# A transformer layer stack with an expert attention branch: a new order of each engine's work in an expert unit, and another opening

## What is computed

```python
xn = _layernorm(x, axis=-1)
x = x + encoder(xn, ...) + expert_attention(xn, ...)
```

```python
qs.append(jnp.einsum('bnm,dm->bnd', xm, q_w[:, :m]) + q_b)     # xm = xn[..., :m], m = d // 2 ** e
...
attn = softmax(einsum('bhqd,bhkd->bhqk', q, k) * scale);  out = einsum(attn, v) -> projection + x
```

## Time and profile before

| what | us |
|---|---|
| runs | 1592.49, 1591.91, 1586.09 (median 1591.91) |
| the profiled execution | 1587.46 |
| its span (first to last instruction) | 1585.5 |
| PE busy in the span | 1413.4 |
| ACT busy | 1219.2 |
| DVE busy | 1089.7 |
| POOL busy | 606.5 |

### The profile page before, as it was taken

The page is one execution under the profiler, slowest core; times in us unless marked ns, Lnnn a source line. Parts: engine busy times, 40 slices in busy tenths (PEclk is TensorE's granted clock), DMA queues, the critical chain, the costliest instruction groups (busy, mean ns, idle before and its releaser), DMA issues.

```text
span 1585.5 us, 39460 instructions
## 1 busy us (share of the span) xinstructions
PE 1413.4 (89%) x10594; PEld 941.7 (59%) x10720; DVE 1089.7 (69%) x2850; ACT 1219.2 (77%) x2165; POOL 606.5 (38%) x1052
## 2 busy tenths in 40 slices
PE   0677778669999999999999999999999999999995
PEld 0445555435666666666666666666666666666653
DVE  6576667456676777777777767767777777777762
ACT  3233333237899999999999989999999999999883
POOL 5232322223334333433333333334333345555433
PEclk9899988779999999999999999999999999999997
DMA  4333332144444444544444445444444554444430
GB/s 127 110 101 100 100 100 89 51 122 121 122 121 125 130 125 128 150 126 120 123 130 127 121 128 152 126 122 131 127 120 131 134 140 129 138 136 127 130 86 11
DMA packets 106534, 187.78 MB, mean 118 GB/s; under 512 B 20104, under 2 KB 72456, under 8 KB 106448
## 3 DMA queue, kind: packets, MB, share of 16 engines
q1 hardware_dynamic: 91632, 150.45, 34.4%
q0 software_dynamic: 14848, 36.72, 8.4%
HBM read 120.87 MB, written 65.01 MB: 117 GB/s over the span
## 4 chain that ended last, share of the span: by engine, by line
PE 69%; DVE 11%; issue 8%; DMA 5%; ACT 3%; POOL 1%; SPq 0%; DVEq 0%; POOLq 0%; ACTq 0%
PE pvp L1079 14%; PE exp_ps L1056 11%; DVE negm L772 10%; PE mxp L1022 10%; PE dense L1120 7%; PE mxp L968 5%; PE dense L997 5%; PE mxp L1026 4%; PE dense L1108 3%; PE dense L968 3%; PE mxp L1007 2%; PE mxp L1097 2%; DMA blocks<-negt 2%; PE mxp L1030 1%; DMA blocks<-split_L 1%
## 5 line engine op out<-in xcount | busy, mean ns | idle before, releaser
L922 ACT ACTIVATE probs<-exp_ps 128x512 f32<-128x512 f32 x896 | 512.1, 592 | 226.2 <-PE exp_ps L1056 221.7
L772 DVE TENSOR_REDUCE negm<-mxp 128x2 f32<-128x512 f32 x896 | 572.4, 686 | 77.3 <-PE mxp L1026 56.6
L1056 PE MATMUL exp_ps<-qbd_l,kst_l 128*128 128x512 f32 x768 | 346.8, 479 | 13.7 <-ACT exp_ps L947 9.7
L1022 PE MATMUL mxp<-blocks,qst 104*128 104x512 f32 x768 | 334.1, 468 | 4.9 <-DMA blocks<-split_L 4.2
L947 ACT ACTIVATE exp_ps<-masktf 128x512 f32<-128x512 f32 x513 | 308.7, 602 | 22.8 <-DVE rest L844 6.5
L596 POOL TENSOR_TENSOR lo<-y,hi 128x512 fp32r<-128x512 f32 x80 | 102.7, 1284 | 344.8 <-DVE hi L747 344.8
L1079 PE MATMUL pvp<-probs,vst_l 128*32 128x256 f32 (+1 forms) x4096 | 208.2, 333 | 10.6 <-issue 10.6
L1026 PE MATMUL mxp<-maskb,identb 128*128 128x256 bf16 (+1 forms) x642 | 197.8, 308 | 0.0
L1022 PEld LDWEIGHTS mxp<-blocks,qst 104*128 104x128 f32 x768 | 148.7, 194 | 46.3 <-issue 29.0
L1079 PEld LDWEIGHTS pvp<-probs,vst_l 128*32 128x32 f32 x4096 | 111.2, 110 | 95.8 <-issue 38.0
L1026 PEld LDWEIGHTS mxp<-maskb,identb 128*128 128x128 bf16 x768 | 75.2, 98 | 150.9 <-issue 137.7
(11 more groups left out here) (99 smaller groups left out, 1927.2 us busy)
## 6 DMA issues: line engine op xcount, KB each, us to landing
split_L<-hi SPq DMA_DIRECT2D x256, 128.0 KB, 2.1
qst<-split_L SPq DMA_DIRECT2D x64, 384.0 KB
kst_l<-split_L SPq DMA_DIRECT2D x64, 384.0 KB
qbd_l<-split_L SPq DMA_DIRECT2D x256, 96.0 KB
split_L<-lo POOLq DMA_DIRECT2D x128, 128.0 KB, 2.3
blocks<-split_L POOLq DMA_DIRECT2D x128, 96.0 KB, 4.3
blocks<-split_L SPq DMA_DIRECT2D x128, 96.0 KB
split_F<-hi SPq DMA_DIRECT2D x64, 128.0 KB, 2.1
```

Source lines behind the costliest of these rows:

```text
L772: dve.tensor_reduce(heads[:, g, first:first + count], bank[MAX_BANK + k % 3].rearrange("p (h t) -> p h t", h=count), AX.X, ALU.max, negate ...
L922: act.activation(probs[:, g, ch, :], exp_ps[:, k % 2, :], ACT.Exp, scale=plan.scale).then_inc(q.b_exp, 1)
L1022: pe.matmul(o, qst[0:BIAS_END, g, qt * P:(qt + 1) * P], kbd[0:BIAS_END, first:first + count, g, 0:keys], start=True, stop=True, skip_group ...
L1056: last = pe.matmul(o, kst[plan.name][:, s, g, kt * P:(kt + 1) * P], rhs, start=seeder not in ("ACT", "DVE"), stop=True, skip_group_check=True)
```

## The change

It has two parts. First, the expert slot is written anew: since each engine picks only its own steps out of the list, the new list gives each engine another order. Second, the opening loads the first quarter and the weights of the projections first, runs the statistics of two quarters and the norm of one, and starts the first unit; the rest is put between the first slots by a list of functions (`between`).

```diff
@@ Plan.slot_steps (two of its new rows)
-            + at("negt negt+ row>", s + 1) + part("pv", s, 2)
-            + part("pv", s, 3) + at("pv+", s) + at("stack> stackp", s + 2))
+                at("rstd ln", s + 2) + at("v+", s + 1) + at("op", s - 2) + at("stack>", s + 1) + at("hi>", s + 2)
+                + at("pv+", s - 1) + at("row> v", s + 1) + at("xn", s + 2) + at("ot+", s - 1) + at("xt+", s + 2)
@@ EXPERT
-    "xt": 1, "qk": 1, "v": 0, "at": 1, "op": 0, "negt": 1, "ot": 4})
+    "xt": 2, "qk": 2, "v": 1, "at": 0, "op": 4, "negt": 3, "ot": 0})
@@ expert_rounds
-    experts(-1)
-    experts(0)
-    experts(1)
+    for k, (n, slots) in enumerate(((-1, (0,)), (-1, (1,)), (0, (0, 1)), (1, (0, 1)))):
+        experts(n, slots=slots)
+        if between[k] is not None:
+            between[k]()
@@ SP
+            load_quarter(0)
+            for dst, src in ((wa["F"], wa_f), (seg_rows, seg_in)):
+                sp.dma_start(dst[:], src).then_inc(s_w_first, 16)
+            sp.dma_start(constant[0], rows_kf).then_inc(s_rows_first, 16)
+            load_quarter(1)
...
+            load_quarter(2)
+            load_quarter(3)
@@ POOL
-            pool.memset(blocks[:].bitcast(F32), 0.0).then_inc(s_zero, 1)
...
-            for k in range(4):
+            for k in range(2):
                 inverse_deviation_of_quarter(k, k + 1)
...
+            def clear_queries(k):
+                pool.memset(qbd["L"][0:ALIBI_ROW, k // 2, 8 * (k % 2):8 * (k % 2) + 8, :].bitcast(F32), 0.0).then_inc(s_initv, 1)
...
+            def second_half_of_deviations():
+                for k in range(2, 4):
+                    inverse_deviation_of_quarter(k, k + 1)
+                clear_queries(0)
...
+            expert_rounds(pool, experts, encoder, join,
+                          (None, second_half_of_deviations, lambda: clear_queries(1), lambda: clear_queries(2)))
@@ DVE
-            dve.memset(qbd["L"][0:ALIBI_ROW, :, :, :].bitcast(F32), 0.0).then_inc(s_initv, 1)
+            dve.memset(blocks[:].bitcast(F32), 0.0).then_inc(s_zero, 1)
...
+            expert_rounds(dve, experts, encoder, join,
+                          (lambda: first_norm(1), second_half_of_statistics, second_half_of_norms, None))
@@ ACT
+            act.wait_ge(s_rows_first, 16)
+            round_rows(0)
+            act.wait_ge(s_w_first, 16 * 2)
...
+            expert_rounds(act, experts, encoder, lambda: wait_for_projections(act, S["F"]),
+                          (round_other_rows, None, None, None))
```

More of the change, by code:

```diff
@@ L108, in slot_steps @@
         return (
[L109 to L115, removed]
-            + at("negt negt+ row>", s + 1) + part("pv", s, 2)
-            + part("pv", s, 3) + at("pv+", s) + at("stack> stackp", s + 2))
+                at("rstd ln", s + 2) + at("v+", s + 1) + at("op", s - 2) + at("stack>", s + 1) + at("hi>", s + 2)
+                + at("pv+", s - 1) + at("row> v", s + 1) + at("xn", s + 2) + at("ot+", s - 1) + at("xt+", s + 2)
+                + at("at+ ot", s - 1) + at("xt", s + 2)
+                + part("exp", s, 0, 1) + at("at", s - 1) + at("qk", s + 2) + part("pv", s, 0) + at("y", s + 2)
+                + at("xb", s - 2)
+                + part("exp", s, 2, 3) + at("op+", s - 2) + at("lo hi", s + 2) + part("max", s + 1, 0)
+                + at("stackp", s + 2) + part("max", s + 1, 1)
+                + part("exp", s, 4) + part("max", s + 1, 2, 3)
+                + part("exp", s, 5, 6) + part("max", s + 1, 4, 5) + part("pv", s, 1) + part("max", s + 1, 6)
+                + part("exp", s, 7) + part("max", s + 1, 7) + part("pv", s, 2, 3) + at("negt+ negt", s + 1))
     def steps(self, n, last_layer=False, slots=(0, 1), early=None):
@@ L224, in wait_for_projections, with expert_rounds @@
         eng.wait_ge(q.lo_parts[s], 16 * 2 * EXPERT.rounds)
-def expert_rounds(eng, experts, encoder, join):
-    experts(-1)
-    experts(0)
-    experts(1)
+def expert_rounds(eng, experts, encoder, join, between=(None, None, None, None)):
+    for k, (n, slots) in enumerate(((-1, (0,)), (-1, (1,)), (0, (0, 1)), (1, (0, 1)))):
+        experts(n, slots=slots)
+        if between[k] is not None:
+            between[k]()
     with eng.Fori(2, EXPERT.rounds - 1) as n:
@@ L673, in encoder, with join @@
                 steps(ENCODER, n, **part_of_round)
-            expert_rounds(pool, experts, encoder, lambda: wait_for_projections(pool, S["F"]))
+            def clear_queries(k):
[4 more added lines that the diff above has]
+                clear_queries(0)
+            def join():
+                clear_queries(3)
+                pool.wait_ge(s_w, 16 * 3)
+                wait_for_projections(pool, S["F"])
+            expert_rounds(pool, experts, encoder, join,
+                          (None, second_half_of_deviations, lambda: clear_queries(1), lambda: clear_queries(2)))
             pool.wait_ge(S["F"].b_s, EXPERT.exp_chunks * GROUPS * EXPERT.units)
@@ L709, in first_norm, with quarter_statistics @@
                     last.then_inc(s_norm, 1)
-            for k in range(4):
+            def quarter_statistics(k):
                 dve.wait_ge(s_x[k], 16)
@@ L714, in _ @@
                 statistics_of_quarter(rest, k, k + 1)
[L715 to L718, removed]
+            quarter_statistics(0)
+            quarter_statistics(1)
+            first_norm(0)
+            dve.wait_ge(s_w_first, 16 * 2)
             def statistics(q, stage, u, s, source):
@@ L882, in join, with second_half_of_statistics, second_half_of_norms @@
                 dve.sem_inc(S["L"].c_done, BATCH)
-            expert_rounds(dve, experts, encoder, join)
+            def second_half_of_statistics():
+                quarter_statistics(2)
+                quarter_statistics(3)
+                dve.wait_ge(s_w, 16 * 3)
+            def second_half_of_norms():
+                first_norm(2)
+                first_norm(3)
+            expert_rounds(dve, experts, encoder, join,
+                          (lambda: first_norm(1), second_half_of_statistics, second_half_of_norms, None))
             dve.wait_ge(S["F"].c_done, BATCH)
@@ L889, in _, with round_rows @@
         def _(act):
[L891 to L895, removed]
+            def round_rows(k):
+                for s in range(2):
+                    stack = (kst["F"], kst["L"], qbd["L"])[k]
+                    act.activation(stack[ALIBI_ROW:P, s, :, :].rearrange("p h t -> p (h t)"), constant[k], ACT.Copy)\
+                        .then_inc(s_rounded, 1)
+            act.wait_ge(s_rows_first, 16)
+            round_rows(0)
+            act.wait_ge(s_w_first, 16 * 2)
             def steps(plan, n, last_layer=False, **part_of_round):
@@ L954, in encoder, with round_other_rows @@
                 steps(ENCODER, n, **part_of_round)
-            expert_rounds(act, experts, encoder, lambda: wait_for_projections(act, S["F"]))
+            def round_other_rows():
+                act.wait_ge(s_rows, 16 * 2)
+                round_rows(1)
+                round_rows(2)
+            expert_rounds(act, experts, encoder, lambda: wait_for_projections(act, S["F"]),
+                          (round_other_rows, None, None, None))
             act.wait_ge(S["F"].c_done, BATCH)
@@ L1143, in _, with others_loaded @@
             pe.wait_ge(s_init, 12)
[L1144 to L1147, removed]
+            pe.wait_ge(s_zero, 3)
+            pe.wait_ge(s_rounded, 2)
+            pe.wait_ge(s_w_first, 16 * 2)
+            def others_loaded():
+                pe.wait_ge(s_rounded, 6)
+                pe.wait_ge(s_w, 16 * 3)
+            expert_rounds(pe, experts, encoder, lambda: wait_for_projections(pe, S["F"]),
+                          (None, others_loaded, None, None))
             pe.wait_ge(s_ones, 1)
```

13 lines of the change are left out of this document (8 added, 5 removed).

## The result

| | median us | range | ratio to before (95%) |
|---|---|---|---|
| before | 1591.91 | 1586.09 to 1592.49 | |
| after | 1578.90 | 1577.21 to 1580.70 | 0.9931 [0.9909, 0.9953] |

What follows compares the result with a forecast made beforehand. No engine was full; a chain of waits and the low clock set the slot. Slots minus 16.1, opening minus 0.9, end plus 1.0 made minus 16.0 us: 1571.5 for the profiled execution, 1575 by the median, range 1560 to 1589.

Steps and rivals of the forecast that it cites:

- The slot at full clock: Expert slot in the new order: 14.7 us against 15.7 at full clock, 1.0 us less.
- The low clock: Expert slots: 1.2 GHz stretches cost the old order 0.5 us a slot; 0.3 us a slot allowed in the new.
- third rival: Slower: PE's 1.4 us hole ahead of `ot` brings 1.2 GHz, 17.1 us a slot, 1607 us in all; chance 0.08.
- `exp` 0 behind `xt`: In the slot, `exp` 0 starts at 4.7 us after `negt` instead of 3.2, waiting for `xn` rather than a transfer.
- `negt` behind `pv` 2 and 3: At the slot's end, `pv` 3 needs `exp` 7, so the transposes come 0.5 us later, 14.7 instead of 14.2.
- The opening: Before the slots: first row of maxima 14.0 us earlier, 12.1 given back by moved work, 1.0 slow start; net -0.9 us.
- The loads hide: In the opening, the first quarter's load has landed when needed; if only at 10.60, the gain shrinks by 3.4 us.
- The end: Into the encoder: older units' `pv+`, `ot`, `op` come ahead of the last `exp` 0; +1.0 us (0 to 3).
- The fourth rival: Second half's norms cost more because DVE and POOL contend for a port: +1 to +3 us, added to the other cases.
- Sum: Whole kernel: slots minus 16.1, opening minus 0.9, end plus 1.0, together minus 16.0 us.
- second rival: No change: the slot only swaps one wait for another, 15.7 us and the low clock stay, 1592 to 1588; chance 0.2.
- signs of being wrong: Slot not shorter at full clock, mean clock of the stretch below 0.85, or the encoder's own stretch changing in length.

Runs made afterwards that it cites:

- e1: The kernel before with only the new slot order and bank table, keeping the old opening: 1578.50 us, ratio 0.994 to before.
- e4: The changed kernel with only POOL's three memsets moved from the slots' borders to just ahead of `lo`: 1579.29 us, ratio 0.994 to before.
- e6: The changed kernel with `xt` behind `exp` 0 and 1 instead of ahead of them: 1585.21 us, ratio 0.9984 to before.
- e7: The changed kernel with the second quarter's load right behind the first's, ahead of weights and rows: 1575.83 us, ratio 0.9927 to before.
- e3: The changed kernel with the second half's work spread one piece per slot, ahead of `hi` (DVE) and `lo` (POOL): 1571.49 us, ratio 0.9896 to before.
- e5: The changed kernel with `negt` ahead of `pv` 2 and 3, as in the old order: 1561.92 us, ratio 0.9843 to before.
- e8: The changed kernel with the edits of e3, e5 and e7 together: 1556.18 us, ratio 0.9794 to before.
- e11: The changed kernel with rounds 2 to 6 written out instead of looped: 1568.51 us, ratio 0.9882 to before.
- e9: e8 with POOL's pieces of the opening also waiting until DVE's `xn` is done: 1550.19 us, ratio 0.9766 to before.
- e10: e1 with `negt` ahead of `pv` 2 and 3, so with the old opening: 1564.52 us, ratio 0.9862 to before.
- e12: e9 with rounds 2 to 6 written out instead of looped: 1546.04 us, ratio 0.9743 to before.

## Why the prediction was right, and where it was off

**The slot at full clock: the mechanism was right, the term too large.** 14.7 us was said, and 14.67 is what the looped slot takes that doesn't contain the loop's jump (in e1, e4, e6 and e7; in after it never ran at full clock). But the 15.70 it was held against is a slot with the jump; that of the same kind in after is 15.10, and the old one without it 15.36. So the gain is 0.6 to 0.7 us a slot, not 1.0; only the written-out slots gain 1.1 (15.42 to 14.35). I had taken one slot as the reference where the loop makes two kinds. In the slot with the jump the count runs 0.3 to 0.4 late from `xn` on: `xn` ends at 4.5 us behind `negt` against 4.1, `qk` starts at 6.3 against 5.9, the reductions end at 14.5 against 14.2.

**The low clock: mis-sized.** I allowed 0.3 us a slot. In the loop it costs 0.98 us in every second slot (15.65 against 14.67), half a microsecond on average, and some 2.5 in the slot that ends at 133.02 (17.25; the same slot took 14.77 at full clock in e3). That is close to the 0.5 that I had read for the old order, where I had counted on less. What runs slow is short, as these rows of after's slow slot show (`exp` 0 and 1, `at`, `qk`, `pv` 0):

```profile
167.45 0.96 PE L1105 MATMUL exp_ps<-blocks,kst_f 128*128 128x512 f32 x2
168.21 0.63 PE L1017 MATMUL dense<-ident,attn 128*128 128x128 f32 x2
168.94 2.07 PE L1046 MATMUL mxp<-xnt,wa_f 128*128 128x256 f32 x4
170.94 1.13 PE L1128 MATMUL pvp<-probs,vst_f 128*32 128x256 f32 x8
```

`at` and `qk` (0.38 and 1.13 at full clock), and a part of the `exp` pair (0.73); `pv` 0 is almost back. So the third rival's mechanism did occur, in most slots at 0.98 us and only in one of after's loop at the full 2.4, and could not turn the sign. Both terms together make the fifteen slots minus 10.9 us, where minus 16.1 was said.

**`exp` 0 behind `xt`: the place was right, its meaning wrong.** It starts 4.8 us after `negt`, as worked out (4.7). "That is the price of the new order: a wait for `xn` replaces a wait for a transfer" is refuted by `e6_xt_later`: with that price taken back the full-clock slot is not shorter. The path runs through `xn`, `xt` and `qk`, which my count of 14.7 had followed all the same.

**`negt` behind `pv` 2 and 3.** I let it come 0.5 late; it comes 0.45 later behind its reductions than in e5 (163.07 - 162.49 against 169.94 - 169.81). The number was right. What the step missed is that in this order the low clock stays: between the first and the sixteenth row, putting `negt` first is worth 12.7 us, not 15 x 0.45 = 6.8.

**The opening: a loan, as said.** First row minus 12.7 (minus 14.0 said), given back 13.1 (13.1 said, with the slow start). The 1.3 us are the step "The loads hide", which it qualified by a loss of up to 3.4: DVE waits 2.20 us for quarter 1, part of it made up by a memset that starts 0.85 us earlier. Where that wait happened to be nothing (e6), the first row came at 41.10, minus 15.0. ACT's rounding, which was to be level with `xnt` of unit 1, is (32.05 and 32.23). The moved work stood bare as worked out: 23.2 us and 20.1 for the two long intervals (22 and 19 said).

**The end.** Plus 0.8 (plus 1.0 said, 0 to 3 as bounds); over the other kernels with the new order 0.4 to 3.0.

**The fourth rival** came only in small in the change. The memsets there stand ahead of `rstd`, where DVE is waiting for it: the `xn` behind the first of them took 0.60. The norms of quarters 2 and 3, which began beside the second, took 4.59 us, in e4 without it 4.17, and the norm of quarter 1 took 3.09 instead of 2.11 beside POOL's `lo`. The full hold of `xn` came as soon as e3, e4 and e8 moved the memsets.

**Sum.** In the profiles: slots minus 10.9, opening plus 0.3, end plus 0.8, and plus 2.8 in the encoder stretch, which the change doesn't touch: minus 6.9, the difference of the spans. The medians differ by 13.0, since the profiled execution of before lay 4.5 us under its median and that of after 1.8 above. That the forecast of 1575 lies only 3.9 off is partly luck of this kind: my sum was minus 16, and without the encoder's drift the rows give minus 9.8. By the rows the change came out some two fifths short of my sum, in the direction of the second rival; the last POOL memset, said for 297 to 298, came at 304.36. One of my signs of being wrong, a change in the encoder's own stretch, did show with these 2.8 us; it was no sign, since that stretch varies by 7.5 us over kernels that leave it alone.

**Left open:** what decides which slots get the low clock. PE's idle time in a full-clock slot is 3.1 us in after (15.11 - 11.98) and 3.0 in e5 (14.68 - 11.70), 4.3 in before; the longest hole is 1.92 us in after, 1.27 in e5. But the length of a slot's own hole doesn't decide it alone: in after's loop the slots with 1.9 us ahead of `ot` ran at full clock and those with 1.55 fell, in e1 it was the other way round, and in e11 the hole was 1.37 in every slot and each third fell. By the rule quoted in the prediction (the Trainium skill, "TensorE: Matmul & The Clock Gate", section "HAM oscillation — how this bites in real kernels") equal slots should all go one way; the trace agrees for the loop slots of e5, e9, e10 and e12 and not for after, where they alternate. Why the loop costs the new order up to 0.8 us a slot and the old one less is also open: in the slot behind the jump DVE's `ln` starts 0.22 us after the row's issue instead of 0.23 ahead of it (the idle time of 0.39 us that the timeline of after puts down to issue), and beside that there are small delays in each slot (`xt` 3.08 us behind the row instead of 2.94 in e11, `qk` 4.77 instead of 4.49, in the slot without the jump). The old order shows the first, 15.70 against 15.36, and not the second. The Trainium skill, "Runtime: NRT & Kernel Launch", section "Instruction fetch mechanics", says that taken branches break the prefetch of instructions and that writing loops out is preferred; e11 and e12 agree with its advice, and no run shows its mechanism.

## What to carry to other kernels

Work moved out of an opening is a loan unless each piece lands where its engine, and those behind it, wait anyway: placed in blocks it gave back 13 of 13 us, in pieces with POOL's held until DVE's `xn` was done it was worth 16. When two orders of a slot are compared, take slots of the same kind (same place in the loop, same clock), and ask of each transposition at the slot's end what stands ahead of it. And count the clock as its own term: putting `negt` first was worth more by the clock (some 7.5 us) than by its path (some 3.5), and no single number of a slot read here said beforehand which slots would fall.

## Seen of the hardware, and not expected

- A POOL memset of 96 x 2048 float32 (1.80 us) holds a pair of DVE tensor_scalar that takes 0.60 us alone and starts up to 0.3 us behind it until its own end (1.69 to 1.92 us, in e3, e4 and e8).
- The low clock can settle on every second of equal slots in a loop, and on every third when they are written out.
- The same slot costs 14.35 us written out and 14.67 or 15.10 looped, all at full clock.
- Sixteen products of `pv` took 1.58 us right behind the score products, with the last exponential ending 0.47 us after the first of them began, and 1.08 when all inputs were ready.
- With the loads issued in the same order, DVE waited between 0 and 2.20 us for the second quarter of the input.
